# Filler matrix products in TensorE's waits: expert stages, both ends of the linear attention, softmax beginning

## What is computed

```python
x = x + 0.5 * _L0_ffn_ref(_layernorm(x), ...)   # 8 experts, top 1, capacity 256, relu
x = x + _L0_attn_ref(_layernorm(x), ...)        # gated linear attention, 16 heads of 8
x = x + 0.5 * _L0_ffn_ref(_layernorm(x), ...)
x = x + 0.5 * _L1_ffn_ref(_layernorm(x), ...)   # 8 experts, top 1, 128 -> 512 -> 128, gelu
x = x + _L1_attn_ref(_layernorm(x), ...)        # softmax attention, masked after the softmax, then layernorm
x = x + 0.5 * _L1_ffn_ref(_layernorm(x), ...)
```

## Time and profile before

| | |
|---|---|
| time, median of 3 runs | 879.61 us (878.43 to 880.32) |
| the profiled execution's own time | 876.03 us |
| its span, first to last instruction | 874.2 us |
| mean granted TensorE clock | 0.882 |
| PE busy | 672.2 us (77%) |
| PEld busy | 347.0 us (40%) |
| DVE busy | 580.9 us (66%) |
| ACT busy | 455.2 us (52%) |
| POOL busy | 332.0 us (38%) |
| chain that ended last | PE 55%, issue 17%, DVE 16%, DMA 5%, POOL 3% |

### The profile page before, as it was taken

How to read it: one execution, slowest core, us unless ns; L and a number is a source line. 1 busy time by engine, 2 the same in 40 slices (tenths; PEclk the granted TensorE clock), 3 DMA queues, 4 the chain that set the end, 5 groups by cost and what they waited for, 6 DMA issues and landing times.

```text
span 874.2 us, 14331 instructions
## 1 busy us (share of the span) xinstructions
PE 672.2 (77%) x4582; PEld 347.0 (40%) x4582; DVE 580.9 (66%) x1141; ACT 455.2 (52%) x872; POOL 332.0 (38%) x767
## 2 busy tenths in 40 slices
PE   4185867545409946899999999999999999952993
PEld 4172322434408934123333434343333423421992
DVE  5436998825533448868788787879978797333343
ACT  2045501223106635047777677867767677851661
POOL 0634564255442423321433324144342344161342
PEclk9997999578558978559999999999999999985897
DMA  8352940044112014620010202020020000011103
GB/s 261 114 155 56 272 70 1 12 128 117 29 58 65 27 54 119 184 57 2 23 34 2 56 1 57 1 57 1 2 56 2 1 2 2 4 34 55 47 28 100
DMA packets 56929, 51.31 MB, mean 59 GB/s; under 512 B 6152, under 2 KB 46804, under 8 KB 56600
## 3 DMA queue, kind: packets, MB, share of 16 engines
q1 hardware_dynamic: 52168, 42.19, 18.7%
q0 software_dynamic: 4544, 7.60, 3.4%
q10 hardware_dynamic: 144, 0.61, 0.3%
HBM read 30.04 MB, written 21.80 MB: 59 GB/s over the span
## 4 chain that ended last, share of the span: by engine, by line
PE 55%; issue 17%; DVE 16%; DMA 5%; POOL 3%; ACT 2%; SPq 2%; POOLq 0%; ACTq 0%; DVEq 0%
PE PS L1080 14%; PE PS L1008 11%; PE PS L1047 11%; PE PS L785 6%; DVE ARENA L1821 6%; PE PS L796 5%; DVE X L1426 2%; DVE XN L1377 2%; DVE STATS L1350 2%; PE PS L757 1%; DMA ARENA<-slots_x 1%; PE PS L735 1%; PE PS L748 1%; POOL slots_x L1875 1%; SPq L541 1%
## 5 line engine op out<-in xcount | busy, mean ns | idle before, releaser
L1821 DVE TENSOR_REDUCE ARENA<-PS 128x1 f32<-128x1024 f32 x256 | 301.0, 1219 | 63.3 <-PE PS L1008 62.5
L1315 ACT ACTIVATE ARENA<-PS 128x512 f32<-128x512 f32 x512 | 273.0, 606 | 78.6 <-PE PS L1047 73.6
L1008 PE MATMUL PS<-ARENA 72*128 72x512 bf16 x512 | 165.5, 407 | 13.7 <-DMA ARENA<-k_parts 7.3
L1047 PE MATMUL PS<-ARENA 75*128 75x512 bf16 x512 | 163.4, 386 | 0.0
L1080 PE MATMUL PS<-ARENA 128*8 128x128 f32 (+8 forms) x1920 | 152.5, 432 | 1.2 <-POOL ARENA L1997 1.0
L1997 POOL TENSOR_SCALAR_AFFINE_SELECT ARENA<-ARENA 128x128 f32<-128x128 f32 x256 | 74.5, 298 | 127.9 <-ACT ARENA L1315 127.6
L1047 PEld LDWEIGHTS PS<-ARENA 75*128 75x128 bf16 x512 | 48.1, 98 | 88.5 <-ACT ARENA L1315 38.8
L1008 PEld LDWEIGHTS PS<-ARENA 72*128 72x128 bf16 x512 | 42.7, 100 | 99.2 <-DVE ARENA L1821 39.8
L1696 DVE TENSOR_TENSOR ARENA<-PS,ARENA 128x512 f32<-128x512 f32 x46 | 31.8, 692 | 68.0 <-PE PS L785 68.0
L1080 PEld LDWEIGHTS PS<-ARENA 128*32 128x32 f32 (+2 forms) x1920 | 43.4, 98 | 77.9 <-issue 43.1
L1905 POOL DMA_INDIRECT tokens_y<-ARENA x46 | 44.7, 972 | 74.9 <-DVE ARENA L1705 73.1
(11 more groups left out here) (188 smaller groups left out, 876.3 us busy)
## 6 DMA issues: line engine op xcount, KB each, us to landing
ARENA<-pack_dram SPq DMA_DIRECT2D x8, 514.0 KB, 13.2
ARENA<-slots_x SPq DMA_DIRECT2D x16, 256.0 KB, 3.8
slots_y<-ARENA SPq DMA_DIRECT2D x32, 128.0 KB, 2.9
ARENA<-q_parts SPq DMA_DIRECT2D x21, 192.0 KB
ARENA<-k_parts SPq DMA_DIRECT2D x21, 192.0 KB
slots_x<-FILL SPq DMA_DIRECT2D x2, 1483.5 KB, 19.5
ARENA<-slots_x SPq DMA_DIRECT2D x10, 258.0 KB, 5.4
k_parts<-ARENA SPq DMA_DIRECT2D x10, 256.0 KB, 3.4
```

The lines of the kernel that those rows point to most:

```text
L1008: ins = nc.tensor.matmul(PS[:, slot + c, :], Q3[0:KQ, G % Q3R, g, i * P:(i + 1) * P], K3[0:KQ, G % Q3R, g, c * 512:(c + 1) * 512], start=T ...
L1047: nc.tensor.matmul(PS[:, bank, 0:w], K3[0:MR + 3, G % Q3R, i, j * P:(j + 1) * P], Q3[0:MR + 3, G % Q3R, i, half * 512:half * 512 + w], sta ...
L1315: nc.scalar.activation(PT[:, n % NPT, 0:w], PS[:, bank_of[x], 0:w], ACT.Exp).then_inc(b_exp, 1)
L1821: nc.vector.tensor_reduce(NM[:, k % 4, i:i + 1], PS[:, slot:slot + 2, :].rearrange("p b n -> p (b n)"), AX.X, ALU.max, negate=True).then_i ...
```

## The change

A helper `fill(bank, count)` issues `count` matrix products of the 128x128 identity with the first 256 columns of the constants, in float32, into a PSUM bank that holds nothing needed at that point. Nothing reads the results. No semaphore is incremented. The calls stand in TensorE's list at fixed places: one of 3 at the start, in `norm_turned`, at the head of `linear` and around `last_sums`, at the head of `soft`, ahead of the attention plan, and one product after each A step that precedes the first B. There are 217 of them: 22 behind the A steps, 195 elsewhere. One wait is new: `state_done` for block 14 ahead of the fill into bank 0.

```diff
+            def fill(bank, count):
+
+                for _ in range(count):
+                    nc.tensor.matmul(PS[:, bank, 0:256], ident, C[:, 0:256], start=True, stop=True)
...
                 if ln == 5:
 
+                    fill(5, 17)
                     pe.wait_ge(z_scaled, GR)
                     turn(3)
                     logits(3).then_inc(logits_done, 1)
                     counts(k, 1, 3, 0)
+                    fill(5, 19)
                 elif kind in ("ffn0", "ffn1"):
+                    fill(5, (0, 0, 14)[k])
                     turn(0)
+                    fill(5, (1, 2, 12)[k])
                     turn(1)
                     logits(0)
                     logits(1).then_inc(logits_done, 1)
+                    if k == 2:
+                        fill(5, 4)
                     turn(2)
...
                         counts(k, 0, 3, 0)
+                        fill(5, 8)
                         turn(3)
                         logits(2)
                     logits(3).then_inc(logits_done, 1)
                     counts(k, 1, 3, P)
+                    fill(5, (15, 14, 30)[k])
...
+                fill(5, 14)
                 for c in range(2):
                     turn(c)
                     features(2 * c)
...
                     sums(n)
+                pe.wait_ge(state_done, B * DH - 1)
+                fill(0, 3)
                 last_sums()
+                fill(0, 3)
                 project(1)
...
+                fill(3, 24)
                 turn(0)
                 turn(1)
...
                 pe.wait_ge(one8_made, 1)
+                fill(3, 12)
...
+                first_key_score = sum(x[0] == "A" for x in plan[:plan.index(("B", 0, 0))])
...
                         ins.then_inc(a_scores, 1)
+                        if n < first_key_score:
+                            fill(7, 1)
...
             pe.wait_ge(early_loaded, 16)
+            fill(5, 3)
             pe.wait_ge(consts_made, 3)
```

## The result

The change made the kernel **slower**: 887.39 us as the median of 6 runs (885.80 to 891.57), against 879.02 of the kernel before beside it (6 runs, 875.61 to 880.34). The ratio is 1.011, with a 95% interval of 1.0085 to 1.0135: a small loss, but clear of the scatter. Forecast were 869.4 us and a range of 860 to 876. The profiled execution took 887.18 us, of which the span is 885.4.

What follows compares the result with a forecast made beforehand. Bound where half clock meets TensorE ending the chain, mostly the softmax's beginning. Terms 6.0 - 0.4 + 0.9 + 1.2 - 0.2 + 0.5 + 0.4 + 1.8 = 10.2 us less: 869.4 us from the median 879.61, range 860 to 876.

Steps and rivals of the forecast that it cites:

- Softmax, 6.0 - 0.4: Softmax's beginning: full clock brings V steps sooner, 6.0 us gained, less 0.4 for a possible clock fall before the A steps.
- The first V: Softmax's beginning: four A steps paced by VectorE at 1.18 us put it near 382.2 for 384.19, 2.0 us gained.
- The V's behind it: Softmax's beginning: at full clock the second falls from 5.90 to 3.06 us, the third from 4.19 to 3.06.
- Rival (c): Whole kernel slower: fillers don't hold the clock, A steps take 1.70 us for 1.18; about 907 or 887 us, chance 0.04.
- rule of under 1%: Whole kernel: clock-ramp penalty under 1% of a typical span, so at most 8.7 us back, 870.9 from the median.
- k=3's logits, 1.2: Last router logits of k=3: turn 1.10 and logits 1.89 us halve after 17 fillers; 1.2 us gained.
- k=2's logits, 0.9: Last router logits of k=2: 16 records from 3.23 to 1.90 us and a faster turn; half taken, 0.9 us.
- the first stage, 0.4: First stage: three fillers and one, before and between the turns, gain 0.4 us, between 0 and 1.9.
- Linear attention's head, "0.2 lost": Linear attention's head: nothing gained because GpSimd's gathers hold VectorE, and a longer pause before the first values; 0.2 us lost.
- the 14 and 12 of k=2: Fillers in k=2's norm, lasting 6.0 and 5.2 us in pauses of 6.8 and 4.3; no net effect expected.
- the 1.8 to be gained at the sorted tokens: Sorted tokens of four expert stages: fillers end too early, clock mostly falls again; 1.8 us gained, between 0 and 10.6.
- prediction's own signs of being wrong: A steps 1.7 us apart, a real product waiting behind fillers on the chain, or gain mainly in the expert stages.

Runs made afterwards that it cites:

- run 1: First probe of marked product groups, some beside indirect gathers, added behind the last stage of the kernel before; the kernel before took 877.14 us in that session.
- run 2: The change without the fillers of the expert stages and the linear attention's head, keeping 17 ahead of k=3's logits, against the kernel before: 871.09 us, ratio 0.9931.
- run 10: The longer probe behind the last stage of the kernel before, in a session where that kernel took 865.14 us; fillers stayed at 0.43 us throughout.
- run 9: Only the fillers meant not to run beside GpSimd's indirect DMAs, against the kernel before at 865.14 us: 857.51 us, ratio 0.9898.
- run 7: The unaltered change repeated in a session where the kernel before took 865.14 us: 856.27 us, ratio 0.9885.
- run 4: The kernel before with only 14 fillers added, behind the counts of k=1 where GpSimd scatters: 879.83 us, one run.
- run 13: The change with bank 5's fillers half as many at 512 columns, plus a seven-phase probe behind the last stage; first A step at 362.93, kernel before 873.60 us.
- the wide and the narrow fillers: The change with bank 5's fillers at 512 or 128 columns, against the kernel before, slower setting: 876.64 us, ratio 1.0026, and 896.24 us, ratio 1.0212.

## Why the prediction was wrong, point by point

- **Softmax, 6.0 - 0.4: right in mechanism, and near in size.** To the fourth V it was 7.5 here, 5.2 between runs 1 and 2, and 4.5 between runs 10 and 9. The clock is at 1.00, the first V comes 29.0 us after the first A for "about 30", and the V's are 3.09 us apart. The parts missed in opposite ways. The first V gained 3.5 where the sum had 2.0, mostly because VectorE's maxima came 1.14 us apart and not 1.18. The V's behind it gained the forecast 3.9 only against the first profile of the kernel before; in runs 1 and 10 the clock of that kernel rose one V earlier, which left 1.6 and 1.0. Rival (c)'s mechanism, fillers that don't hold the clock and A steps 1.7 us apart, did not occur, though its time (887) is that of the result.
- The rule of under 1% that the prediction set against its sum (the Trainium skill, "TensorE: Matmul & The Clock Gate", section "Part 1: The HAM clock gate") agrees with the softmax alone, 7.5 us of 876 or 0.9%. The whole change gave back 1.15% in the faster setting, with an interval of 0.8 to 1.5 that holds 1%: the runs don't decide.
- **k=3's logits, 1.2: right in kind**: the turn took 0.63 and the logits 1.06 for 1.10 and 1.89; the 17 fillers ended before them. It isn't sure to come: in run 2 the turn took 0.63, and the logits 1.88 again.
- **k=2's logits, 0.9, and the first stage, 0.4: wrong.** The 16 records ran at half clock as before, in the faster setting too (3.42 us at 227.50 in run 7), and those of the first stage took 3.42 at 13.71, as they did before:

```profile
258.01 3.42 PE L682 MATMUL PS<-C,XNT 128*128 128x8 f32 x16
```

- **Linear attention's head, "0.2 lost": this is the step that failed**, and with it the "so nothing" for the 14 and 12 of k=2 and the 1.8 to be gained at the sorted tokens. All three cost a filler at 0.43 or 0.85 us and took it as harmless if it ended before the next real product's data. At the head, and ahead of k=2's first turn, the fillers do end in time, and still the semaphore of the product behind them comes 9.3 and 10.7 us late (5 us in run 4). It is some 17 to 21 us in all, where the sum had -0.2 + 1.8 and nothing. One of the prediction's own signs of being wrong, a real product behind fillers on the chain, came true at k=2.
- What was overlooked: most rows of the kernel before show TensorE idle or nearly so while GpSimd scatters and gathers, so the cost of dense work there wasn't known from them. The end of k=1's experts is a place with dense work, and there a report is 2.3 us late, as shown above. The cost should have been bounded from both sides, not taken from rows in which no indirect DMA ran.
- **The clock at the sorted tokens**: as forecast it mostly fell again (the turns of 194.03 and 283.06 took 1.94 us for 8 records), but this isn't where the time went.
- The mean clock rose by 0.055, and the time with it: a warm clock is no gain in itself.
- Where the kernel before takes 865 us, the change gives 8.9 us of the 10.2 that were forecast. By the profiles of runs 10 and 7, 3.4 of them lie ahead of the first A step and 4.5 from there to the fourth V. The first number is near the sum for that stretch partly by luck, since two of its terms brought nothing.

Open: what the slower setting is. The shares of the DMA queues read alike in both (18.5% and 19.0% in the largest queue for the change); two things differ. The kernel before itself is 10 to 13 us slower: in run 10, which is the kernel before up to its probe, the same instructions of VectorE come 3.6 us earlier at 81, 6.1 at 235 and 9.6 at 394 than in the first profile, so most of it lies at the stretches with indirect DMAs, and 3 us at the softmax's beginning. And the trace of such a run has no landing times for them, here the issues of the scatters by the kernel before, in its first profile, and by the change in run 7:

```profile
slots_x<-XN,SCATI POOLq DMA_INDIRECT x32
```
```profile
slots_x<-XN,SCATI POOLq DMA_INDIRECT x32, 2.3
```

So records of semaphore changes are missing there, which fits a backlog on the way of such reports, but doesn't prove one. Every execution here was recorded with its span and clock; whether the marks would be late in one that isn't recorded was not tried. Scatters were tried only in the kernel, not in the probe. And each version met a setting in one to three sessions only, with the wide and the narrow fillers in the slower one in different sessions.

## What to carry to other kernels

A filler isn't free because it ends before the next real data: what counts is when the semaphore of the real product behind it arrives. Put fillers where they keep the clock for products on the chain. Keep them away from stretches in which GpSimd issues indirect DMAs and another engine waits for TensorE. If they must stand there, take few wide products instead of many narrow ones (1.9 us lost for 12.3). When a change gains in one session and loses in another, run the kernel before beside it each time, and look at the place of the loss before the sum.

## What the runs showed of the hardware

- Beside GpSimd's indirect DMAs, in one of two settings, TensorE's semaphore increments came late once some 22 to 32 product records had been issued: in steps of 0.7 and 1.4 us, in bursts, and all at once when the DMAs were over (14 in 1.40 us). In the changed kernel, and in two phases of run 13, TensorE's own issue then stuttered in the same steps. VectorE's and ScalarE's reports beside them were in time (0.06 us before TensorE's turn at 76.28 and 0.03 us before VectorE's use at 74.90 in the changed kernel). In run 13 products of 512 float32 columns, 40 records in 19.3 us, did not run into it; 80 records in 19.2 us did.
- The same chip showed both settings, 877 and 865 us for the same kernel, a difference of 1.4%, more than the change itself brings in either.
- A product of the identity with constants behind each A step, one every 1.14 us, kept the clock at 1.00 with TensorE busy for 9.2 us of 10 (the windows from 372 on). Without it, at 7.18 of 10, it stayed at 0.50.
